# Four engines of a fused attention, fast-weight and FFN layer leave out waits for semaphore values that they have waited for already

## What is computed

```python
x = x + layernorm(attn(layernorm(x)))        # attn = (ttt_out + sliding-window attention) @ Wo
x = x + layernorm(ffn(layernorm(x)))         # ffn = gelu(x @ proj1.T + b1) @ proj2.T + b2
# ttt_out: scan over 4 chunks of 128 tokens, per (batch, head) three 64x64 fast weights W0, W1, W2
def step(carry, xi):
    hid, gate = q @ W2.T, silu(q @ W0.T);  out = (gate * hid) @ W1.T
    gba, hbm = k @ W0.T, k @ W2.T;  sg = silu(gba)
    dhidden = v @ W1
    dw1 = v.T @ (sg * hbm * l1);  dw0 = dgba.T @ (k * l0);  dw2 = dhbm.T @ (k * l2)
    M = dw + M * mean(mom)                                   # for each of the three
    for a, b, c in NS_COEFFS:                                # 5 Newton-Schulz rounds on M / |M|
        A = X @ X.T;  B = b * A + c * (A @ A);  X = a * X + B @ X
    W = renorm(W + X)
```

## Time and profile before

| | us |
|---|---|
| median of 3 runs | 379.28 (378.91 to 379.86) |
| the profiled execution | 379.39 |
| its span on the core | 377.6 |
| TensorE matmul busy | 369.0 (98%) |
| TensorE weight loads busy | 294.4 (78%) |
| VectorE busy | 256.9 (68%) |
| ScalarE busy | 212.1 (56%) |
| GpSimd busy | 193.9 (51%) |

### The profile page before, as it was taken

The page is one execution under the profiler, slowest core; times in us unless marked ns, Lnnn a source line. Parts: engine busy times, 40 slices in busy tenths (PEclk is TensorE's granted clock), DMA queues, the critical chain, the costliest instruction groups (busy, mean ns, idle before and its releaser), DMA issues.

```text
span 377.6 us, 15942 instructions
## 1 busy us (share of the span) xinstructions
PE 369.0 (98%) x6754; PEld 294.4 (78%) x6754; DVE 256.9 (68%) x676; ACT 212.1 (56%) x429; POOL 193.9 (51%) x289
## 2 busy tenths in 40 slices
PE   8989999999999999999999999999999999999994
PEld 7577788756888878878577888689887757988883
DVE  4688998582478699898547746987875492767124
ACT  2889865756603765649733446665357575614500
POOL 5499666354248656485963524364333440557211
PEclk9999999999999999999999999999999999999998
DMA  7652100002000000000000200000000110000101
GB/s 261 241 176 88 43 2 5 3 3 59 3 3 2 3 2 3 4 4 3 17 17 17 71 16 3 2 2 17 19 4 4 40 37 2 0 3 0 57 0 56
DMA packets 9685, 12.22 MB, mean 32 GB/s; under 512 B 912, under 2 KB 8720, under 8 KB 9616
## 3 DMA queue, kind: packets, MB, share of 16 engines
q1 hardware_dynamic: 9616, 11.22, 9.1%
HBM read 9.12 MB, written 2.10 MB: 30 GB/s over the span
## 4 chain that ended last, share of the span: by engine, by line
PE 88%; DVE 5%; POOL 2%; issue 2%; ACT 2%; POOLq 0%; DVEq 0%; ACTq 0%
PE pair L776 15%; PE pair L787 15%; PE pair L553 7%; PE pair L695 6%; PE pair L685 6%; PE pair L707 6%; PE pair L676 5%; PE pair L757 3%; PE pair L562 3%; PE pair L585 3%; PE pair L726 3%; PE pair L742 3%; PE pair L656 2%; PE pair L733 2%; PE pair L623 1%
## 5 line engine op out<-in xcount | busy, mean ns | idle before, releaser
L776 PE MATMUL pair<-xn2T,p1T 128*128 128x512 f32 (+1 forms) x160 | 59.1, 512 | 0.0
L787 PE MATMUL pair<-p2T,h 128*128 128x256 f32 x256 | 57.0, 379 | 0.0
L787 PEld LDWEIGHTS pair<-p2T,h 128*128 128x128 f32 x256 | 48.0, 190 | 6.4 <-issue 0.2
L1408 POOL TENSOR_SCALAR var<-mv 128x1 f32<-128x1 f32 (+1 forms) x54 | 13.0, 242 | 63.6 <-DVE mv L1363 35.0
L1029 ACT ACTIVATE h<-pair,packed_in 128x512 f32<-128x512 f32 (+1 forms) x40 | 23.9, 602 | 36.1 <-PE pair L776 36.1
L776 PEld LDWEIGHTS pair<-xn2T,p1T 128*128 128x128 f32 x160 | 28.7, 190 | 17.1 <-issue 14.7
L1403 POOL TENSOR_TENSOR nq<-ssq,half 128x8 f32<-128x8 f32 (+1 forms) x16 | 24.2, 1512 | 26.5 <-DVE ssq L1135 26.5
L1051 DVE SCALAR_TENSOR_TENSOR A<-pair,eye 128x512 f32<-128x512 f32 x45 | 28.8, 683 | 13.0 <-PE pair L685 12.7
L1403 POOL TENSOR_TENSOR rstd<-var,neg_half 128x1 f32<-128x1 f32 (+1 forms) x55 | 33.4, 607 | 7.1 <-DVE var L1366 2.5
L1051 DVE SCALAR_TENSOR_TENSOR B<-pair,eye 128x512 f32<-128x512 f32 x45 | 28.9, 684 | 10.0 <-PE pair L695 9.9
L982 ACT ACTIVATE masked<-masked,nmax 128x256 f32<-128x256 f32 (+1 forms) x32 | 15.1, 472 | 26.6 <-DVE nmax L1292 26.6
(11 more groups left out here) (165 smaller groups left out, 771.6 us busy)
## 6 DMA issues: line engine op xcount, KB each, us to landing
x_in<-in_L_attn_x_dram SPq DMA_DIRECT2D x16, 128.0 KB, 2.5
x<-in_L_attn_x_dram SPq DMA_DIRECT2D x16, 128.0 KB, 2.1
out_dram<-rows_a SPq DMA_DIRECT2D x16, 128.0 KB, 1.7
p1T<-in_L_ffn_proj_dram SPq DMA_DIRECT2D x1, 1024.0 KB, 5.0
p2T<-in_L_ffn_proj_dram SPq DMA_DIRECT2D x1, 1024.0 KB, 7.5
W<-in_states_dram SPq DMA_DIRECT2D x1, 768.0 KB, 6.7
wqkv<-in_Wall_dram SPq DMA_DIRECT2D x1, 512.0 KB, 3.9
WT<-in_states_dram SPq DMA_DIRECT2D x1, 512.0 KB, 6.4
```

Of the source, the lines that this page charges most:

```text
L776: mm_ = pe.matmul(ps[:, at], p1T[:, k, n * P:(n + 1) * P], xn2T[:, k, at], start=(k == 0), stop=(k == KC - 1))
L787: mm_ = pe.matmul(ps[:, 0:DIM], h[:, n, b * P:(b + 1) * P], p2T[:, n, :], start=(n == 0), stop=(n == HC - 1))
```

## The change

Each of the four engines gets an object that remembers, per semaphore, the highest value already waited for, and issues a wait only when the asked value is higher. A wait for zero or less is not issued either. All `wait_ge` calls of the four engines go through it, except those inside `wait_apart`. `take_pair` merges two waits for one semaphore into the higher one. SyncE is as before, and no instruction other than waits is added, removed or moved.

```diff
+class Unmet:
+
+    def __init__(self, eng):
+        self.eng, self.met = eng, {}
+
+    def wait_ge(self, signal, n):
+        if n > self.met.get(signal, 0):
+            self.met[signal] = n
+            self.eng.wait_ge(signal, n)
...
         @block.tensor
         def _(pe):
+            unmet = Unmet(pe)
...
                 if last is not None:
-                    pe.wait_ge(*last)
+                    unmet.wait_ge(*last)
                 return BANK[bank]
...
                 one, other = free(bank, signal, c, n), free(bank + 1, signal, c, n)
+                if one is not None and other is not None and one[0] is other[0]:
+                    one, other = (one[0], max(one[1], other[1])), None
                 if one is not None:
-                    pe.wait_ge(*one)
-                if other is not None and other != one:
-                    pe.wait_ge(*other)
+                    unmet.wait_ge(*one)
+                if other is not None:
+                    unmet.wait_ge(*other)
...
-                pe.wait_ge(*S["XT"](c, 3 * it + g + 1))
+                unmet.wait_ge(*S["XT"](c, 3 * it + g + 1))
```

More of the change, by code:

```diff
@@ L548, in QK @@
             def QK(bank, c, b):
-                pe.wait_ge(ld_qkv, 16)
+                unmet.wait_ge(ld_qkv, 16)
                 ps = take(bank[0], "qk_raw", c, b + 1)
-                pe.wait_ge(*(S["xnT"](c, 2) if c else S["first_xnT"](0, b + 1)))
+                unmet.wait_ge(*(S["xnT"](c, 2) if c else S["first_xnT"](0, b + 1)))
                 for k in range(KC):
@@ L556, in VV @@
             def VV(bank, c, b):
-                pe.wait_ge(ld_v, 16)
+                unmet.wait_ge(ld_v, 16)
                 ps = take(bank[0], "v_raw", c, b + 1)
-                pe.wait_ge(*(S["xnT"](c, 2) if c else S["first_xnT"](0, b + 1)))
+                unmet.wait_ge(*(S["xnT"](c, 2) if c else S["first_xnT"](0, b + 1)))
                 for k in range(KC):
@@ L590, in GB @@
                 if bp == 0 or c == 0:
[L591 to L592 removed]
+                    unmet.wait_ge(*(S["ttt_T"](c, 4) if c else S["ttt_T"](0, 2 * bp + 4)))
+                    unmet.wait_ge(*(S["WT"](c, 3) if c else (ld_wT, 32)))
                 for y_ in range(2):
@@ L603, in DH @@
                 take_pair(bank[0], "dh", c, 1)
-                pe.wait_ge(*S["ttt_T"](c, 6 if c else 2))
-                pe.wait_ge(*(S["W"](c, 1) if c else (ld_w, 16)))
+                unmet.wait_ge(*S["ttt_T"](c, 6 if c else 2))
+                unmet.wait_ge(*(S["W"](c, 1) if c else (ld_w, 16)))
                 for b in range(BATCH):
@@ L771, in F1 @@
                 if c == 0 and n == 0:
-                    pe.wait_ge(ld_p1, 16)
+                    unmet.wait_ge(ld_p1, 16)
                 if n == 0:
-                    pe.wait_ge(*S["xn2T"](c, 2 if part == 0 else 4))
+                    unmet.wait_ge(*S["xn2T"](c, 2 if part == 0 else 4))
                 for k in range(KC):
@@ L782, in F2 @@
                 if c == 0 and b == 0:
-                    pe.wait_ge(ld_p2, 16)
+                    unmet.wait_ge(ld_p2, 16)
                 if new:
-                    pe.wait_ge(*S["h"](c, HC if b == 0 else 2 * HC))
+                    unmet.wait_ge(*S["h"](c, HC if b == 0 else 2 * HC))
                 for n in range(HC):
@@ L808, in _ @@
         def _(act):
+            unmet = Unmet(act)
             def copy(dst, src):
@@ L1067, in LN1 @@
                     return
-                dve.wait_ge(*S["x_in"](c, 64))
-                dve.wait_ge(*(S["xT_ps"](c, 0) if c > 1 else S["first_xT"](0, BATCH)))
+                unmet.wait_ge(*S["x_in"](c, 64))
+                unmet.wait_ge(*(S["xT_ps"](c, 0) if c > 1 else S["first_xT"](0, BATCH)))
                 for b in range(BATCH):
@@ L1492, in WON @@
             def WON(c, b):
-                pool.wait_ge(*S["wo_n"](c, b + 1))
+                unmet.wait_ge(*S["wo_n"](c, b + 1))
                 if b == 0:
-                    pool.wait_ge(*S["x_again"](c, 64))
+                    unmet.wait_ge(*S["x_again"](c, 64))
                 tt(x1[:, c % 2, b, :], wo_n[:, b, :], x1[:, c % 2, b, :], ALU.add).then_inc(S["x1"].sem, 1)
```

390 lines of the change are left out of this document (196 added, 194 removed).

## The result

The changed kernel took 381.20 us (median of 8 runs, 380.22 to 382.38), the kernel before 379.19 us on the same chip (8 runs, 378.80 to 379.86): ratio 1.0051, interval 1.0038 to 1.0063. That is 2.0 us slower. I had forecast 378.3 us, in a range up to 379.4, and had given "slower" 5 in 100.

A forecast was written before the change was run, and what follows sets the result against it. TensorE was taken as the bound, its matmuls busy 98% of the span; gains of 0.56 + 0.05 + 0.16 + 0.19 = 0.96 us, rounded up to 1.0, gave 378.3 us, range 377.5 to 379.4.

The forecast's parts named there:

- The bound, and the met waits: TensorE sets the pace; waits met before, 294 on TensorE and most on the other engines, cost 0 behind queued work.
- Last waits of TensorE, 0.56 + 0.05: Seven last waits on the chain move into the instruction, 0.08 us each; one more at 167.31 us gives 0.05.
- ScalarE and VectorE, 0.16: Fast-weight step at 127.6 and 232.0 us: shorter waits at L909 and L1174 give 0.08 us each time.
- the pause, 0.19: VectorE's standstill at 165.12 us between BN_AGGR and L1109 should go: 0.19 us, up to 0.27, at least nothing.
- rival D: Links off the chain shorten too and count where the chain moves there: 0.3 to 0.6 us more, 377.8; chance 0.08.
- The sum: All gains along the chain: 0.56 + 0.05 + 0.16 + 0.19 = 0.96 us, 1.0 with half of a doubtful 0.08.
- a pause as at 165.12 turns up at another place of the chain: Sign of being wrong: a standstill like VectorE's 0.19 us between BN_AGGR and L1109 appears elsewhere on the chain.
- rival C: Slower: shifted engine work collides on VectorE's part of the chain, 0.7 us each; three collisions give 380.4; chance 0.06.
- A with one collision: Shortened links uncover other limits, 0.3 us gained (chance 0.17), plus one 0.7 us VectorE collision; taken as upper bound, 379.4.

The follow-up runs named there:

- the turned version: Kernel before, all waits kept; on all four engines the unmet wait is written first and goes into the instruction: 377.23 us, ratio 0.9946.
- The pads: Kernel before with 48 separate waits for a value long reached added to TensorE's program near 35.4 us: 384.24 us, ratio 1.0134.
- the variant with only these turned: Kernel before, all waits kept; on TensorE alone the unmet wait is written first and goes into the instruction: 378.69 us, ratio 0.998.
- turned on the three engines: Kernel before, all waits kept; on ScalarE, VectorE and GpSimd alone the unmet wait goes into the instruction: 378.26 us, ratio 0.9968.
- the changed kernel's second trace: The changed kernel run and profiled once more, nothing altered: 380.90 us, ratio 1.0041 to the kernel before.
- the variant with 8 waits for VectorE: Changed kernel with 8 separate waits for a value long reached at the start of VectorE's program: 380.39 us, ratio 1.0028 to the kernel before.

## Why the prediction was wrong

*The bound, and the met waits.* Right. TensorE paces the kernel and the waits that were met cost nothing where it has work queued: with the four engines' 408 + 232 + 221 + 97 separate waits all kept, the turned version is the fastest of all. The pads put a limit to it: in a row, with nothing queued, a separate instruction with two met waits costs 0.11 us, not the 0.02 to 0.05 that I gave.

*Last waits of TensorE, 0.56 + 0.05.* Right in mechanism (0.14 became 0.04), and the size agrees as far as it is known: the variant with only these turned gained 0.8 us by the ratio, interval 0.2 to 1.3, and 0.25 by its one profiled span, in which the two short pauses at block ends took some 0.4 us.

*ScalarE and VectorE, 0.16, and the pause, 0.19.* The pause went: L1125 starts 0.07 us after BN_AGGR does, and L1109 started 0.34 after, so 0.27 us. With the waits turned and VectorE's program as long as before, the same instruction starts 0.24 us after BN_AGGR. So 0.10 of the 0.27 us was the form of the wait; the other 0.17 stayed with the position or the separate instruction ahead, and which of the two was not tested. The links were too few: turned on the three engines the waits gave 1.2 us in all (0.8 to 1.7). That fits rival D, links beside the chain that I followed; I did not trace them one by one.

*The sum.* 1.0 us, and 1.01 is what the changed kernel gained outside the two stops. It agrees better than its parts, and that closely it is luck: by the same reckoning the changed kernel's second trace gives about 1.1 us and the variant with 8 waits for VectorE 1.4.

*The step that failed* is the sentence on what else the change moves. I wrote of VectorE that "the instructions behind it move to other places in the instruction stream" and counted this as a gain at one place; for TensorE I put down the 294 instructions at zero and did not ask where its block ends would go. They moved by 142 positions at 165 us and 294 at the end, and brought 1.57 us of stops and 0.46 us in the last transfer: 2.03 against 1.01 gained, +1.0 of span, as measured (378.6 less 377.6). The medians are further apart, by 2.0 us. A likely reason is that the stops are not of one length (in the traces the distance at 6594 is 0.40 to 1.12 us and at 7619 0.98 to 1.26), but the runs without a trace do not show it.

*The warning signs.* I had one of my own: "a pause as at 165.12 turns up at another place of the chain". And the last sentence of rival C, "a moved pause of 0.19 to 0.27 us", had the kind of event right and the size wrong by a factor of four, since I took it from VectorE, whose short programs need a block once in some 50 us, while TensorE's 64-wide steps need one every 2 us. The collisions of rival C are not what happened. One sum was off as well: A with one collision gains 0.3 us and loses 0.7, so it ends at 379.7 and not at the 379.4 that I took as the upper bound; the 381.20 us measured lie beyond both.

*The page that I cited.* The Trainium skill (Runtime: NRT & Kernel Launch, Instruction fetch mechanics) gives blocks of 256 instructions and calls the crossing mostly hidden. The trace agrees for TensorE on the block (16,384 bytes, a stop only every 256 positions) and on "mostly" (51 of 53 block ends after). I used the page to argue that the pause at 165 was no crossing, because q14's packets are 8 KB. That argument fails: for VectorE the block is just half as long, and the pause sits at instruction 448 of its program, 64 + 3 x 128, a block end. That it was a crossing is not shown either, since the q14 packet near it starts at 165.81 us, after the pause.

## What to carry to other kernels

Number the instructions of the engine that sets the pace. In the 64-wide steps here it ran through a block of 256 in 2.2 to 2.4 us, and the next block was not there sooner than about 2.3 us after its fetch started. Then any edit ahead of it, even leaving out what costs nothing, can put 1 us stops into a step or take them away. Compare two versions at equal program length before you believe a difference under 1%, and look at the block ends in their traces even so: two of the turned versions had pauses of 0.23 to 0.27 us there at equal length.

If a wait has to be fast, write it so that it goes into the instruction, and let the met ones be the separate ones: here that alone gave 2.0 us, and no instruction changed its position.

## What the runs showed of the hardware

- TensorE's stops at block ends: 0.40 to 1.62 us, 23 times, each ending 2.28 to 2.93 us after the start of the packet. Its block ends lie at 192 + 256k. The 15 and 14 packets of q14 fit ends at 64 + 128k for the other three engines.
- A packet of 8 KB of instructions on q14 among an output's 144 packets made the last one start 1.69 us after the issue in place of 1.34 (1.53 with the other three engines' change alone), and the signal came 0.3 to 0.5 us later.
- Separate wait instructions with two waits each, in a row on TensorE: 0.11 us each, at a duration of 0.05.
- At the start of the program matmuls of 32 columns and of 128 columns took the same 0.21 us a record, in a stretch in which 512-wide ones took 0.85 us and not the 0.43 of later.
